# A four-layer attention and feed-forward network on one core: GpSimd's root, the entry and the block order of a wide attention with its MLP, and the order of the attention's last units

## The reference

```python
ik = input_seq @ Wk + bk
mk = state_seq @ Wk + bk
iv = input_seq @ Wv + bv
mv = state_seq @ Wv + bv
q = jnp.einsum('bmd,hdp->bhmp', state_seq, Wq) + bq[None, :, None, :]
inp_score = jnp.einsum('bhmp,bsp->bhms', q, ik)
self_score = jnp.sum(q * mk[:, None], axis=-1, keepdims=True)
score = jnp.concatenate([self_score, inp_score], axis=-1)
score = score / jnp.sqrt(jnp.asarray(p_, jnp.float32))
attn = jax.nn.softmax(score, axis=-1)
v_in = jnp.einsum('bhms,bsp->bhmp', attn[..., 1:], iv)
v_self = attn[..., 0:1] * mv[:, None]
heads = (v_in + v_self).transpose(0, 2, 1, 3).reshape(b_, m_, h_ * p_)
attn_out = heads @ Wo + bo
x1 = _layernorm(attn_out + state_seq, g1, b1)
mlp = jax.nn.relu(x1 @ Wg + bg) * (x1 @ Wl + bl) @ Wm + bm
return _layernorm(mlp + x1, g2, b2)
```

## Time and profile before

| what | value |
|---|---|
| median of 3 runs | 775.16 us (774.05 to 778.88) |
| the profiled execution, its own time | 773.79 us |
| its span in the trace | 772.0 us |
| TensorE busy | 714.9 us, 93% |
| VectorE, ScalarE, GpSimd busy | 520.0, 459.2, 419.8 us |
| TensorE clock over the span | 0.993 of full speed |
| wide attention, from unit 0's queries to the transposes of its last sums | 185.36 to 354.78 us |
| its MLP, to the end of the second output | 355.35 to 381.52 us |

### The profile page before, as it was taken

The page is one execution under the profiler, slowest core; times in us unless marked ns, Lnnn a source line. Parts: engine busy times, 40 slices in busy tenths (PEclk is TensorE's granted clock), DMA queues, the critical chain, the costliest instruction groups (busy, mean ns, idle before and its releaser), DMA issues. The chain is left out here.

```text
span 772.0 us, 14614 instructions
## 1 busy us (share of the span) xinstructions
PE 714.9 (93%) x5071; PEld 578.7 (75%) x5071; DVE 520.0 (67%) x1380; ACT 459.2 (59%) x1388; POOL 419.8 (54%) x414
## 2 busy tenths in 40 slices
PE   6989999998899999898989999979889899999896
PEld 3657887776788887776877788756668788888796
DVE  6888666676766666576656677668866266666566
ACT  3993456664877776663134777479924356666322
POOL 6875157774666644534122677467640388786311
PEclk9999999999999999999999999999999999999999
DMA  7003032220000000000004345100020332210000
GB/s 289 7 2 151 1 125 83 82 69 1 2 1 2 8 2 1 1 2 1 8 22 128 130 130 155 70 2 2 3 68 1 98 110 69 82 56 1 1 0 28
DMA packets 16360, 38.45 MB, mean 50 GB/s; under 512 B 1896, under 2 KB 6272, under 8 KB 16032
## 3 DMA queue, kind: packets, MB, share of 16 engines
q1 hardware_dynamic: 16288, 37.53, 14.7%
HBM read 36.87 MB, written 0.66 MB: 49 GB/s over the span
## 5 line engine op out<-in xcount | busy, mean ns | idle before, releaser
L1369 PE MATMUL banks<-input_hi,weights_in_lo 128*128 128x512 f32 x296 | 120.7, 408 | 6.7 <-PEq L1770 2.1
L1369 PE MATMUL banks<-input_lo,weights_in_hi 128*128 128x512 f32 x296 | 115.9, 392 | 0.0
L1369 PE MATMUL banks<-input_hi,weights_in_hi 128*128 128x512 f32 x296 | 115.7, 391 | 0.0
L1080 ACT ACTIVATE probabilities<-banks,neg_max 128x128 f32<-128x128 f32 x256 | 91.0, 465 | 12.7 <-DVE neg_max L2140 12.6
L899 POOL TENSOR_TENSOR hidden_lo<-hidden,hidden_hi 128x512 fp32r<-128x512 f32 x50 | 64.6, 1296 | 38.8 <-ACT hidden L1239 35.4
L727 POOL TENSOR_TENSOR rstd<-var_eps,neg_half 128x4 f32<-128x4 f32 x23 | 23.8, 1033 | 98.3 <-POOLq L726 85.5
L1080 ACT ACTIVATION_READ_ACCUMULATOR probabilities<-banks,neg_max 128x1 f32 x256 | 72.9, 305 | 0.0
L1369 PEld LDWEIGHTS banks<-input_hi,weights_in_lo 128*128 128x128 f32 x296 | 55.8, 189 | 21.8 <-DVE hidden_lo L2504 3.4
L906 POOL TENSOR_TENSOR hidden<-hidden,scratch 128x512 f32<-128x512 f32 x48 | 62.0, 1295 | 18.1 <-ACT hidden L1225 15.9
L1369 PE MATMUL banks<-hidden_hi,weights_out_lo 128*128 128x512 f32 x164 | 67.6, 412 | 1.5 <-POOL weights_out_lo L889 1.2
L856 POOL TENSOR_TENSOR weights_in_lo<-weights_in,weights_in_hi 128x256 fp32r<-128x256 f32 (+2 forms) x30 | 37.7, 1258 | 56.2 <-ACT weights_in_hi L1250 55.3
(11 more groups left out here) (300 smaller groups left out, 1839.7 us busy)
## 6 DMA issues: line engine op xcount, KB each, us to landing
scratch<-cw_rows SPq DMA_DIRECT2D x25, 512.0 KB, 3.7
weights_out<-w_in SPq DMA_DIRECT2D x17, 256.0 KB, 2.7
weights_in<-w_in SPq DMA_DIRECT2D x8, 512.0 KB, 3.8
weights_in<-w_in SPq DMA_DIRECT2D x9, 256.0 KB, 2.7
weights_in<-w_in SPq DMA_DIRECT2D x16, 128.0 KB, 2.2
weights_out<-w_in SPq DMA_DIRECT2D x16, 128.0 KB, 2.1
wq<-w_in SPq DMA_DIRECT2D x1, 1024.0 KB, 5.2
wo<-w_in SPq DMA_DIRECT2D x1, 1024.0 KB, 7.5
```

Of the source, the lines that this page charges most:

```text
L1080: act.activation(prob[:, n // 2 % 2, h, :], b8(n % (2 if prune else 3))[:, i, :], ACT.Exp, bias=neg_max8[:, n % 4, i:i + 1], accum_out=z[: ...
L1369: return pe.matmul(o, l, rh, start=start, stop=stop, **kw)
```

## The change

In the wide block, by engine:

- **GpSimd:** the root of step 27 goes from the front of the step's list to a place behind `self_values` and `self_products`.
- **TensorE, entry:** `turn_state` moves from step 0 to step 1 and `state_rest` from the end of step 1 to that of step 2; the state's keys go to bank 6 instead of 3. **ScalarE:** the tokens are taken behind `copy_own` and `queries` of step 1, and the keys are evacuated in step 2. **VectorE:** `state_values` moves to step 3, behind `weights` of unit 0.
- **Last units:** values of units 30 and 31 go to banks 0 and 1 and stand ahead of `turn_heads` in their steps; turned heads of unit 31 go to bank 2, without the wait for the low part of unit 30. `enter_mlp` moves one step up on TensorE and ScalarE. On VectorE the weights of units 30 and 31 stand ahead of `heads_out`, the low parts of units 28 to 31 come one step later, and therewith behind the next unit's `heads_out`; the split of the MLP's first half comes in step 35 instead of 37, and the second `scale` in step 31 instead of 32. Unit 31's output issues its two products with the high part before it waits for the low part.
- **MLP:** banks (k + half) % 3; the transposes of half 1 go between two groups of three filler products ahead of the fourth block of half 0; the first block of half 1 is issued ahead of the first output; one filler stands before that output instead of four. ScalarE takes half 1's input before the fourth block, VectorE splits it before the fourth gate.

The other feed-forward parts keep their order and banks.

```diff
-                return k % 3 if self.gated else (self.FC * n + k) % 4
+                return (k + n) % 3 if self.gated else (self.FC * n + k) % 4
...
-                return (1, 0)
+                return (0, 3) if self.gated else (1, 0)
...
+        def values_bank(n):
+            return 4 if n < 30 else n - 30
+
+        def headsT_bank(n):
+            return 5 if n < 31 else 2
...
-                pipelined(pool, [(lambda it, n: inverse_roots((0,)), (15,), 12), (self_values, range(32), 4),
-                                 (self_products, range(32), 1),
+                pipelined(pool, [(self_values, range(32), 4), (self_products, range(32), 1),
+                                 (lambda it, n: inverse_roots((0,)), (15,), 12),
...
-                act.activation(qT[:, half * 512:(half + 1) * 512], bank[2 + half][:, :], ACT.Identity,
+                act.activation(qT[:, half * 512:(half + 1) * 512], bank[2 + 4 * half][:, :], ACT.Identity,
...
-                pipelined(act, [(take_tokens, (1,), 0), (enter_mlp, (0,), 35),
-                                (copy_probsT, range(32), 3), (exps, range(32), 2), (copy_own, range(32), 1),
-                                (queries, range(32), 0), (evacuate_state_keys, (1,), 0),
+                pipelined(act, [(copy_probsT, range(32), 3), (enter_mlp, (0,), 34),
+                                (exps, range(32), 2), (copy_own, range(32), 1),
+                                (queries, range(32), 0), (take_tokens, (1,), 0),
+                                (evacuate_state_keys, (1,), 1),
...
-                    project(w("wk1"), xnT, 2, (1,), projected_act)
+                    project(w("wk1"), xnT, 5, (1,), projected_act)
...
-                        m = mm(b4(4)[:, i, :], probT[:, 0, 4 * (n % 2) + i, :], iv[:, n // 16 * 4 + i, :])
+                        m = mm(b4(values_bank(n))[:, i, :], probT[:, 0, 4 * (n % 2) + i, :], iv[:, n // 16 * 4 + i, :])
...
-                    if n > 0:
+                    if 0 < n < 31:
                         pe.wait_ge(headsT_ready, n)
...
-                    pe.wait_ge(headsT_ready, n + 1)
-                    m = split_products(bank[6][:, :], lambda part: head_part((wo_lo, wo_hi)[part], h),
-                                       lambda part: (headsT_lo, headsT_hi)[part][:, n % 2, :],
-                                       h == 0, h == H - 1)
+                    if n < 31:
+                        pe.wait_ge(headsT_ready, n + 1)
+                        m = split_products(bank[6][:, :], lambda part: head_part((wo_lo, wo_hi)[part], h),
+                                           lambda part: (headsT_lo, headsT_hi)[part][:, n % 2, :],
+                                           h == 0, h == H - 1)
+                    else:
+                        pe.wait_ge(headsT_hi_ready, n + 1)
+                        mm(bank[6][:, :], head_part(wo_lo, h), headsT_hi[:, n % 2, :], start=False, stop=False)
+                        mm(bank[6][:, :], head_part(wo_hi, h), headsT_hi[:, n % 2, :], start=False, stop=False)
+                        pe.wait_ge(headsT_ready, n + 1)
+                        m = mm(bank[6][:, :], head_part(wo_hi, h), headsT_lo[:, n % 2, :], start=False, stop=True)
...
-                pipelined(pe, [(queries, range(32), 0), (turn_state, (0,), 0), (own_sums, range(32), 1),
-                               (output, range(32), 6), (turn_heads, range(32), 4), (turn_own, range(32), 1),
-                               (values, range(32), 3), (turn_sums, (15, 31), 7), (turn, range(32), 2),
-                               (scores, range(32), 0), (state_rest, (0,), 1), (enter_mlp, (0,), 34)],
+                pipelined(pe, [(queries, range(32), 0), (turn_state, (0,), 1), (own_sums, range(32), 1),
+                               (output, range(32), 6), (values, (30, 31), 3), (turn_heads, range(32), 4),
+                               (turn_own, range(32), 1), (values, range(30), 3), (turn_sums, (15, 31), 7), (turn, range(32), 2),
+                               (scores, range(32), 0), (state_rest, (0,), 2), (enter_mlp, (0,), 33)],
...
                             if half == 0:
-                                keep_busy(6, 5)
+                                keep_busy(6, 3)
+                                transpose_half(1, source, f.entry_bank(1))
+                                keep_busy(6, 3)
                             pe.wait_ge(h_ready, 1)
+                        if f.gated and (half, fc) == (1, 0):
+                            pe.wait_ge(h_ready, 2)
...
-                    keep_busy(6 + half if f.gated else 7, 4 + 5 * (half and f.gated))
+                    keep_busy(6 + half if f.gated else 7, (1, 9)[half] if f.gated else 4)
...
                 hidden(0)
-                transpose_half(1, source, f.entry_bank(1))
+                if not f.gated:
+                    transpose_half(1, source, f.entry_bank(1))
+                else:
+                    hidden(1, (0,))
                 output(0)
-                hidden(1)
+                hidden(1, range(1 if f.gated else 0, f.FC))
...
-                pipelined(dve, [(heads_out, range(32), 4), (weights, range(32), 3), (state_values, (0,), 2),
-                                (maxima, range(32), 1), (low_headsT, range(32), 4), (second_tokens, (0,), 2),
+                pipelined(dve, [(weights, (30, 31), 3), (heads_out, range(32), 4), (weights, range(30), 3),
+                                (state_values, (0,), 3),
+                                (maxima, range(32), 1), (low_headsT, range(28), 4),
+                                (low_headsT, range(28, 32), 5), (lambda it, n: split_input(0), (0,), 35), (second_tokens, (0,), 2),
                                 (residual, (15, 31), 7),
-                                (lambda it, n: split_input(0), (0,), 37),
                                 (statistics, (0, 2), 23), (variance, (0,), 26), (centre, (0, 2), 27),
-                                (scale, (0, 2), 30)], 32, 1, st.close)
+                                (scale, (0,), 30), (scale, (2,), 29)], 32, 1, st.close)
...
-                    for fc in range(f.FC):
+                    for fc in range(3):
                         gate(0, fc)
                     split_input(1)
+                    gate(0, 3)
```

More of the change, by code:

```diff
@@ L1142, in round_headsT @@
                     act.wait_ge(headsT_done, n + 1)
-                    act.activation(headsT_hi[:, n % 2, :], bank[5][:, :], ACT.Copy).then_inc(headsT_hi_ready, 1)
+                    act.activation(headsT_hi[:, n % 2, :], bank[headsT_bank(n)][:, :], ACT.Copy).then_inc(headsT_hi_ready, 1)
                 def queries(it, n):
@@ L1685, in ffn, with hidden @@
             def ffn(f, source):
-                def hidden(half):
+                def hidden(half, blocks=range(f.FC)):
                     if half == 0:
@@ L1689, in hidden @@
                         pe.sem_inc(w_in_ready[0], -1)
-                    pe.wait_ge(input_ready, 1)
-                    pe.sem_inc(input_ready, -1)
+                    if blocks[0] == 0:
+                        pe.wait_ge(input_ready, 1)
+                        pe.sem_inc(input_ready, -1)
                     tokens = slice(half * 512, (half + 1) * 512)
-                    for fc in range(f.FC):
+                    for fc in blocks:
                         if f.gated and fc == 3:
                             if half == 0:
-                                keep_busy(6, 5)
+                                keep_busy(6, 3)
+                                transpose_half(1, source, f.entry_bank(1))
+                                keep_busy(6, 3)
                             pe.wait_ge(h_ready, 1)
+                        if f.gated and (half, fc) == (1, 0):
+                            pe.wait_ge(h_ready, 2)
                         at_bank = f.hidden_bank(half, fc)
@@ L2273, in low_headsT @@
                     dve.wait_ge(headsT_hi_ready, n + 1)
-                    dve.tensor_tensor(headsT_lo[:, n % 2, :], bank[5][:, :], headsT_hi32[:, n % 2, :],
+                    dve.tensor_tensor(headsT_lo[:, n % 2, :], bank[headsT_bank(n)][:, :], headsT_hi32[:, n % 2, :],
                                       ALU.subtract).then_inc(headsT_ready, 1)
@@ L2304, in heads_out @@
                     for i in range(4):
[L2305 removed]
+                        dve.scalar_tensor_tensor(heads[:, n % 2, i, :], b4(values_bank(n))[:, i, :],
                                                  r[:, 0, 4 * (n % 4) + i:4 * (n % 4) + i + 1],
```

3 lines of the change are left out of this document (1 added, 2 removed).

## The result

The changed kernel took 766.16 us (median of four executions, 765.37 to 770.77), the kernel before beside it 774.61 (773.79 to 778.88): ratio 0.9887, interval 0.9855 to 0.9918, that is -8.45 us or -1.1%. The forecast was 769.0 in a range of 766.0 to 772.2 and "within 1%", that is not to be told from no change. The time lies in the range, 2.8 us under the forecast, but the change stands clear of none, so the outcome that the forecast held likeliest (0.84) did not come. The profiled execution after took 765.37 with a span of 763.6, 8.42 less than that of before.

The account below looks back on a forecast made before the run. TensorE's in-order queue, busy 93% of the span, was taken as the bound. Entry -1.2, root -2.9, tail -2.3 and MLP +0.2 sum to -6.2 us: 767.6 profiled, 769.0 as median with 1.37 carried over; range 766.0 to 772.2.

Parts of the forecast that it names:

- within 1%: Whole kernel: the outcome held likeliest, a time not to be told from no change; chance 0.84.
- Entry, -1.2: Attention's start: scores first and an earlier VectorE sum bring unit 3's own sums forward; -1.2 us, bounds -0.5 and -2.1.
- Root, -2.9: Step 27: GpSimd's root placed last removes TensorE's 2.88 us idle; -2.9 us, bounds -2.95 and -2.0.
- Tail, -2.3: Last units, steps 33 to 35: reordering shortens the three-engine loop, sums' transposes earlier; -2.3 us, bounds nothing and -4.5.
- Rival B: Tail only shuffled: the three-engine loop closes again elsewhere, half the tail and only the entry's first part; 770.9 us, chance 0.12.
- MLP, +0.2: MLP: first output slightly later, second still 12.2 us behind it; +0.2 us, bounds -0.2 and +2.5.
- with hardly a hole: MLP second half: a VectorE chain from the first output's end sets the second output, 12.2 us behind the first.
- Rival A: MLP: GpSimd keeps the shared port, VectorE's split waits for the second addition; +2.45 instead of +0.2, 771.2 us, chance 0.14.
- Rival D: MLP: TensorE's clock falls as idle grows and fillers go; slower, up to 780 us, chance 0.03.
- Behind the MLP nothing is edited: After the MLP: next weights load on the MLP's own releases, so the whole -6.2 us should arrive.
- rival C: Behind the MLP, 393 to 396: the low-clock stretch goes away, 1.3 us more won; 767.7 us, chance 0.10.
- A measurement tells about 1%: Whole kernel: only a change of about 7.75 us, to 767.4, can be told from none; faster 0.13, slower 0.03.

Follow-up runs that it names:

- f2: The changed kernel without its MLP edits (entry, root and tail only): 766.99 us, ratio 0.9882 to the kernel before.
- g1: The changed kernel with VectorE's gate of the second half's first MLP block issued ahead of the first residual and output: 767.04 us, ratio 0.9883.
- e1: The kernel before with the entry edits alone: 773.74 us, ratio 0.9978.
- f1: The whole changed kernel run once more, nothing else altered: 767.50 us over six executions, ratio 0.9895 to the kernel before.
- the first four experiments: The kernel before with one part each, entry, root, tail or MLP edits: 773.74, 773.64, 772.14 and 775.26 us.
- g2: The kernel before with only GpSimd's root moved, run a second time: 772.27 us, ratio 0.9946.
- e4: The kernel before with the MLP's new order and banks alone: 775.26 us, ratio 0.9995.
- e3: The kernel before with the edits of the last units (tail) alone: 772.14 us, ratio 0.9961.
- g4: The kernel before with six and seven more filler products in TensorE's two waits behind the MLP, step 27 unfilled: 775.42 us, ratio 1.0002.

## Why the prediction was right in its sum and wrong in its verdict

**Entry, -1.2.** Right: -1.12 at unit 3's own sums, -1.25 alone. A wait at the head outputs of unit 1 did come (0.16 at 207.74; forecast: up to 0.1 taken back).

**Root, -2.9.** Right: -2.92 in the whole change, -3.05 alone. The order of the rows on GpSimd is the forecast one.

**Tail, -2.3.** Right, and so in its stations. Taking the 4.13 of entry and root off the forecast's times gives 340.7 for unit 29's transposes (measured 340.95, released by unit 28's low part, as forecast), 343.7 for unit 30's (343.88), 345.1 for unit 31's (345.33), 348.3 for the sums' (348.59). The 0.37 at unit 28's measured 0.28. Rival B, that the tail is only shuffled, is out.

**MLP, +0.2.** Right in the whole: -0.05 alone, about +0.1 as the difference between the change and f2. The first output is 10.79 behind the sums (forecast 10.9), the second 12.13 behind the first (forecast 12.2). What the forecast put as a chain "with hardly a hole" had a gate that could go earlier (g1, 0.78 us). Rival A, that GpSimd keeps the port, is out: the split did not wait for the second addition. The Trainium skill, "SBUF — State Buffer", section "Who interferes with whom", has whoever issues first hold the shared pair for its whole instruction. The rows agree in that the split took 0.83 instead of 0.69 beside an addition that had started before it, and the next addition 0.50 more than before; they add that the waiting VectorE instruction went ahead of GpSimd's next.

**Rival D**, the clock falling in the MLP, is out: from 340 to 400 no window of the profile after is below 1.00.

**The sum arrived; the failed step is the one after it**: "Behind the MLP nothing is edited ... so all of it should arrive", taken as a flat hand-over of 6.2 us, with 1.37 us added for the distance between the profiled execution and the median. Of the 2.8 us by which the median came under the forecast, 1.0 is the draw of four executions (766.16, where ten have 767.19) and 1.8 are left. Two things were missed.

(1) The clock is not a constant of the kernel. I held one profiled execution for the kernel and looked at one place of low clock, at 393, as rival C with a chance of 0.10; the same profile has others, at 509 and at its end. Between the two profiled executions rival C is what happened. It may be a draw, since kernels without the whole change are found with the stretch and without it. But it may be in part the entry's: of the twelve profiles whose waits there weren't filled, the five with the entry's edits (after, e1, f1, f2, g1) have no stretch behind the MLP, and five of the seven others have one. No run tests that. From the second transposes behind the MLP to the turn of att_tok in the next block the profile of before takes 99.43 us (392.85 to 492.28), after 97.38 (386.65 to 484.03). The other profiles with the stretch there take 98.1 to 98.7, those without 97.3 to 98.2. So that of before was a long one, and 2.05 of the 2.2 us are here. A part of it is a wait of VectorE for a DMA, 2.38 us before and 1.48 after:

```profile
484.51 0.75 DVE L2493 SCALAR_TENSOR_TENSOR hidden<-banks,cols,scratch 128x512 f32<-128x512 f32 x1 [2.38 <-DMA scratch<-cw_rows]
```

```profile
475.99 0.75 DVE L2517 SCALAR_TENSOR_TENSOR hidden<-banks,cols,scratch 128x512 f32<-128x512 f32 x1 [1.48 <-DMA scratch<-cw_rows]
```

The same wait was 1.2 to 1.6 us in the first four experiments, and 2.0 and 2.2 in g1 and g2, so that it varies by itself.

(2) The wait that the change removes had a second price, which the profile of before didn't show: the stretch of 1.6 us behind it in some executions. The median of before carries it, the profiled execution doesn't. Taking 6.2 us off the median, as the forecast does by carrying the 1.37 over, leaves that price in: the 66 executions of before have a median of 775.4, less 6.2 is 769.2, and ten of the changed kernel have 767.2. An offset as such is not the mistake: these ten lie 1.8 above the changed kernel's own profiled execution. The mistake is in the size, not the sign: the root's term was the idle time alone (2.9), and in the mean over executions it comes with up to the 2.2 us that filling the wait gave.

**A second step failed beside it**: "A measurement tells about 1% (7.75 us, 767.4) from no change", from which came 0.84 for "within". The measured interval reaches 0.32% to each side. With that width the forecast's own -6.2 us, 0.8%, would already have stood clear of no change. So a gain clear of no change followed from the forecast's own sum, and the 2.2 us on top were not needed for it. What they did was to bring the change to the 1% line itself, which lies inside the interval (0.8% to 1.5%).

**What stays open.** The stretch at 318 alone explains at most 0.6 x 1.6, about 1.0 us of the 2.2. By the mean clock the rest comes as fewer stretches elsewhere. The one at 739 to 745 came in two of the five profiles with the unfilled wait at step 27 and in none of the nine others, which may be chance; nothing here shows why a wait at step 27 should matter 420 us later. Removing the wait alone raised the clock by 0.0016, filling it by 0.0031; with 19 and 12 executions these may still be one value. And the tail alone raised it by 0.0015 with that wait in place. So that the change raises the mean clock is shown, and that a filler at step 27 does; how the gain is shared between the root, the tail and the entry is not.

## What to carry to other kernels

An in-order TensorE made the parts add: where each was worked out from the row that it removes to the row that then ends last, four terms came out within 0.25 us each. Before a profiled execution's offset from the median is carried over, ask what the offset is made of; the mean clock of each execution tells it, and one profile holds only one draw of the short stretches at half clock. Set the width of the interval that the measurement will have against the forecast change before saying that it can't be told from none. Price a wait of some 3 us on TensorE at its length and, beside it, at a stretch that may follow; where the wait must stay, filler products that end before the releaser may win that part (here 0.3% for one line).

## What was not expected of the hardware

Around 2.88 us without a product TensorE's granted clock fell to 0.50 in three of five profiles, and stayed at 1.00 in two: two of each (before and e4; e3 and g4) ran the same instructions up to there, so it doesn't follow from the program alone. Nor does the fall have one distance from the wait: it came over 1 us into the following work in e1 and e3, and 0.2 us before the wait's end in g4, where 317 to 318 is granted 0.90 and 318 to 319 0.50 and the own sums start at 317.98. At 739 in e4 it came with TensorE's last idle row 9.6 us in front (729.36). From the own sums to those two steps on, the stretch at 318 costs 1.64, 1.64 and 1.45 us (e1, e3, g4). Ten filler products in the wait changed the time of the whole kernel by 1.9 us in the median with the transposes behind the MLP at 207.40 us instead of 207.49.
